# Row terms of the attention scores: GpSimd products and ScalarE sums in place of single-column TensorE products

## The reference, cut to what matters

```
c  = layernorm(x)                                   # 8 batches x 64 tokens x 512 features
cq = einsum('bcd,bqd,d->bcq', c, q, w_cq) + b_cq    # q: 8 x 512 x 512
s  = (c @ w_c + b_c)[:, :, None] + (q @ w_q + b_q)[:, None, :] + cq
a  = softmax(s, axis=2)                             # over q
c2q_att = einsum('bcq,bqd->bcd', a, q)
b_att = softmax(max(s, axis=2), axis=1)             # over the tokens
q2c_att = einsum('bc,bcd->bd', b_att, c)[:, None, :]
z = concat([c, c2q_att, c * c2q_att, c * q2c_att]) @ W_l.T + b_l
```

## Time and profile before

| what | value |
|---|---|
| median of 3 runs | 463.41 us (462.15 to 463.58) |
| the profiled execution's own time | 460.11 us |
| its span, first to last instruction | 458.3 us |
| TensorE busy | 431.9 us, 94% of the span |
| VectorE, ScalarE, GpSimd busy | 277.6, 162.8, 50.9 us |
| mean granted clock of TensorE | 0.985 |

### The profile page before, as it was taken

How to read it: one execution, slowest core, us unless ns; L and a number is a source line. 1 busy time by engine, 2 the same in 40 slices (tenths; PEclk the granted TensorE clock), 3 DMA queues, 4 the chain that set the end, 5 groups by cost and what they waited for, 6 DMA issues and landing times.

```text
span 458.3 us, 8060 instructions
## 1 busy us (share of the span) xinstructions
PE 431.9 (94%) x3103; PEld 310.7 (68%) x3112; DVE 277.6 (61%) x552; ACT 162.8 (36%) x316; POOL 50.9 (11%) x59
## 2 busy tenths in 40 slices
PE   1999999999999999999998999999999999999991
PEld 1666566689898899977467766666666666666660
DVE  5759697673454224488678866654456664446637
ACT  4335234123332114432335432355533355533100
POOL 1300000003221111110203300000000000000064
PEclk9999999999999999997999999999999999999996
DMA  7998795006999766006033769999999999984454
GB/s 266 403 387 327 255 415 201 1 1 250 407 406 405 278 239 246 3 1 245 34 124 154 222 190 375 371 305 338 342 349 361 359 352 327 344 314 146 169 156 137
DMA packets 52382, 116.95 MB, mean 255 GB/s; under 512 B 4834, under 2 KB 4850, under 8 KB 52352
## 3 DMA queue, kind: packets, MB, share of 16 engines
q1 hardware_dynamic: 25984, 67.12, 38.6%
q10 hardware_dynamic: 24800, 44.62, 27.9%
q0 software_dynamic: 1568, 4.79, 3.2%
HBM read 93.98 MB, written 21.50 MB: 252 GB/s over the span
## 4 chain that ended last, share of the span: by engine, by line
PE 88%; DVE 6%; DMA 2%; issue 2%; ACT 1%; POOL 1%; DVEq 0%; ACTq 0%; POOLq 0%
PE banks L1793 19%; PE banks L1559 10%; PE banks L1770 6%; PE banks L1772 6%; PE banks L1771 6%; PE banks L1420 4%; PE banks L1642 3%; PE banks L1422 3%; PE banks L1407 3%; PE banks L1459 3%; PE banks L1421 3%; PE banks L1388 3%; PE banks L1782 2%; PE banks L1592 2%; PE banks L1539 2%; PE banks L1541 2%
## 5 line engine op out<-in xcount | busy, mean ns | idle before, releaser
L1793 PE MATMUL banks<-w,A 128*128 128x512 f32 x208 | 91.6, 592 | 0.0
L674 ACT ACTIVATE A<-banks,b_sb 128x128 f32<-128x128 f32 x112 | 30.5, 384 | 110.7 <-issue 76.7
L1793 PEld LDWEIGHTS banks<-w,A 128*128 128x128 f32 x208 | 38.5, 190 | 43.1 <-issue 43.0
L1292 DVE COPY A<-banks 128x512 f32<-128x512 f32 x28 | 18.0, 686 | 66.9 <-PE banks L1772 66.7
L1220 DVE TENSOR_TENSOR w_lo<-w,w_hi 128x1024 fp32r<-128x1024 f32 x48 | 55.4, 1216 | 0.0
L607 ACT ACTIVATE w_hi<-w 128x1024 fp32r<-128x1024 f32 x48 | 47.3, 1089 | 1.1 <-ACT A L674 0.8
L1559 PE MATMUL banks<-A,w 128*128 128x128 f32 x384 | 46.6, 277 | 0.0
L1559 PEld LDWEIGHTS banks<-A,w 128*128 128x128 f32 x384 | 44.1, 192 | 0.8
L1770 PE MATMUL banks<-w_hi,xr 128*128 128x512 f32 x100 | 40.1, 401 | 0.6 <-DVE xr L1237 0.6
L1771 PE MATMUL banks<-w_lo,xr 128*128 128x512 f32 x104 | 40.5, 389 | 0.0
L1772 PE MATMUL banks<-w_hi,xr 128*128 128x512 f32 x100 | 39.0, 390 | 0.0
(11 more groups left out here) (288 smaller groups left out, 738.2 us busy)
## 6 DMA issues: line engine op xcount, KB each, us to landing
w<-in_w SPq DMA_DIRECT2D x12, 2048.0 KB, 10.1
w<-in_w ACTq DMA_DIRECT2D x12, 2048.0 KB, 10.4
rows_dram<-att ACTq DMA_DIRECT2D x1, 14592.0 KB, 43.0
A<-in_ctxT SPq DMA_DIRECT2D x8, 1024.0 KB, 10.3
A<-in_ctx SPq DMA_DIRECT2D x8, 1024.0 KB, 9.2
w<-in_w SPq DMA_DIRECT2D x6, 1024.0 KB, 5.2
rows_dram<-A ACTq DMA_DIRECT2D x13, 256.0 KB, 3.3
w<-in_wlT SPq DMA_DIRECT2D x3, 1024.0 KB, 14.8
```

Source lines behind the costliest of these rows:

```text
L674: ins = nc.scalar.activation(hT[:, u, f, :], HT[f // 4][:, tile(f % 4)], ACT.Gelu, bias=b1_sb[:, u, f:f + 1])
L1793: ins = mm(YP[:, :], hT[:, u, f, :], w2[:, u, f * D:(f + 1) * D], start=(f == 0), stop=(f == FT - 1))
```

## The change

GpSimd loads `w_c` once as a row on all 128 partitions (256 KB). For each tile it multiplies the normed tile `cn` by it into a scratch that lies in the later `wqkv` buffer. ScalarE sums each scratch tile along its row with an Identity activation in place and its accumulator. VectorE's `token_sums` takes that sum. TensorE's `row_terms` is gone, and with it one 2 KB load on ScalarE's queue. The sum of tile 0 stands between `widen_first` and `copy_cT(0, 1)`; the sums of tiles 1 to 3 stand together between `high_wl(7)` and `exp_scores(1)`. The four products stand on GpSimd ahead of its parameter loads. The `wqkv` load, whose buffer holds the scratch, waits for the four sums too.

```diff
-SCORE_PARAMS = 4
+SCORE_PARAMS = 3
...
+        wc_row, wc_terms = A2[:, 7680:8192], wqkv_flat[:, 3072:5120].rearrange("p (t d) -> p t d", t=NT)
...
             sp.wait_ge(first_psum, NT)
+            sp.wait_ge(rows_summed, NT)
             sp.dma_start(wqkv[:, :, :], ...
...
-            act.dma_start(wc[:, :], t["wcT"]).then_inc(score_params_in, 16)
...
+            def sum_row_terms(n):
+
+                act.wait_ge(terms_ready, n + 1)
+                nc.scalar.activation(wc_terms[:, n, :], wc_terms[:, n, :], ACT.Identity,
+                                     accum_out=row_sum[:, n:n + 1]).then_inc(rows_summed, 1)
...
             widen_first()
+            sum_row_terms(0)
             copy_cT(0, 1)
...
             high_wl(7)
+            for n in range(1, NT):
+                sum_row_terms(n)
             exp_scores(1)
...
+            pool.dma_start(wc_row, t["wc"].to_broadcast([P, D])).then_inc(wc_in, 16)
+            pool.wait_ge(wc_in, 16)
+            for n in range(NT):
+                pool.wait_ge(normed, n + 1)
+                nc.gpsimd.tensor_tensor(wc_terms[:, n, :], cn[:, n, :], wc_row, ALU.mult).then_inc(terms_ready, 1)
+
             pool.wait_ge(s_psum, 1)
...
-                dve.wait_ge(r_psum, n + 1)
+                dve.wait_ge(rows_summed, n + 1)
                 dve.wait_ge(nmax_ready, n + 1)
-                link(nc.vector.scalar_tensor_tensor(msum[:, n:n + 1], nmax[:, n:n + 1], -1.0, MI[:, 0:1],
+                link(nc.vector.scalar_tensor_tensor(msum[:, n:n + 1], nmax[:, n:n + 1], -1.0, row_sum[:, n:n + 1],
...
-            def row_terms(n):
-
-                if n:
-                    pe.wait_ge(q2c_taken, n)
-                else:
-                    pe.wait_ge(score_params_in, 16 * SCORE_PARAMS)
-                for k in range(KT):
-                    ins = mm(MI[:, 0:1], cT[:, k, tile(n)], wc[:, k:k + 1], start=(k == 0), stop=(k == KT - 1))
-                ins.then_inc(r_psum, 1)
...
-            row_terms(0)
...
-            row_terms(1)
...
-                    row_terms(n + 1)
```

More of the change, by code:

```diff
@@ L80, in perceiver_kernel @@
         slot_row = before
-        wcq = sb("wcq", [P, KT]); wq = sb("wq", [P, KT]); wc = sb("wc", [P, KT])
+        wcq = sb("wcq", [P, KT]); wq = sb("wq", [P, KT])
         scal = sb("scal", [P, 3]); bsum = sb("bsum", [P, 1])
@@ L162, in perceiver_kernel @@
         nmax = sb("nmax", [P, NT]); asum = sb("asum", [P, NT]); arec = sb("arec", [P, NT])
-        msum = sb("msum", [P, NT])
+        msum = sb("msum", [P, NT]); row_sum = sb("row_sum", [P, NT])
         mT = sb("mT", [1, 2, S]); mmax = sb("mmax", [1, 2]); msb = sb("msb", [1, 2])
@@ L223, in perceiver_kernel @@
         first_psum = sem("first_psum")
+        wc_in, terms_ready = sem("wc_in"), sem("terms_ready")
         wqkv_in, conv_in, wo_in, params_in = map(sem, ("wqkv_in", "conv_in", "wo_in", "params_in"))
@@ L230, in perceiver_kernel @@
         consts, pool_step = sem("consts"), sem("pool_step")
-        dve_step, act_step = sem("dve_step"), sem("act_step")
+        dve_step = sem("dve_step")
         normed, var_ready, root_ready = sem("normed"), sem("var_ready"), sem("root_ready")
         cT_psum, cT_ready, cw_ready = sem("cT_psum"), sem("cT_ready"), sem("cw_ready")
-        s_psum, nmax_ready, exp_done, r_psum = map(sem, ("s_psum", "nmax_ready", "exp_done", "r_psum"))
+        s_psum, nmax_ready, exp_done, rows_summed = map(sem, ("s_psum", "nmax_ready", "exp_done", "rows_summed"))
         aT_psum, aT_ready, cq_psum, c2q_ready = map(sem, ("aT_psum", "aT_ready", "cq_psum", "c2q_ready"))
@@ L1848, in _ @@
                 ins.then_inc(last_psum, 1)
-_NAMES = ["x", "ctx", "ctxT", "wcqT", "wqT", "wcT", "b_cq", "b_c", "b_q", "wlT", "b_l", "wqkvT", "qkv_bT", "convT",
+_NAMES = ["x", "ctx", "ctxT", "wcqT", "wqT", "wc", "b_cq", "b_c", "b_q", "wlT", "b_l", "wqkvT", "qkv_bT", "convT",
           "conv_bT", "woT", "out_b", "gateT", "w1", "b1T", "w2", "b2"]
@@ L1868 @@
         "ctxT": np.asarray(ctx_1024).transpose(0, 2, 1),
-        "wcqT": by_feature(L0_xattn_w_cq), "wqT": by_feature(L0_xattn_w_q), "wcT": by_feature(L0_xattn_w_c),
+        "wcqT": by_feature(L0_xattn_w_cq), "wqT": by_feature(L0_xattn_w_q), "wc": np.asarray(L0_xattn_w_c).reshape(1, D),
         "b_cq": np.asarray(L0_xattn_b_cq).reshape(1, 1), "b_c": np.asarray(L0_xattn_b_c).reshape(1, 1),
```

## The result

The changed kernel takes 466.00 us (median of 6 runs, 465.35 to 467.17) against 462.96 us (6 runs, 461.87 to 463.58) on the same chip: ratio 1.007, 95% interval 1.0052 to 1.0088, slower by 3.0 us. The forecast was +0.5 us. Its range of 461.8 to 465.8 missed the median by 0.2 us, and 0.63 stood on "within 0.3%". The profiled execution took 466.0 us, its span is 464.2 us.

A forecast was written before the change was run, and what follows sets the result against it. TensorE was 88% of the chain, but a load set `scores(3)`. Delays 0.4 + 0.7 + 0.35 less tile 3's 0.98 gave +0.47 us on 460.11; adding 3.30 for the median gave 463.9 us, range 461.8 to 465.8.

The forecast's parts named there:

- part 6: Loads from `attend(1)` to `scores(3)`: the queue runs at its full rate, so `ctxT(3)` is delayed by as much as `attend(1)`.
- part 1: Products removed from TensorE, 2.94 us at most: tile 1's becomes some 0.4, tile 2's nothing, tile 3's the full 0.98 us.
- Rival D: TensorE idle from 20.1 to 22 us drops its clock to 0.50, costing 3 us more: 466.9; chance 0.05.
- the signs to look for: Expected in the profile after: TensorE idle over 1 us before 22 us and 0.6 before `att` transposes; `scores(3)` waiting over 1.
- Part 4, product 0: GpSimd's first product, 9.2 to 10.4 us, delays `low_part(0, 0)`; it or the row's load makes `scores(0)` late: +0.4 us.
- Part 4, products 1 to 3: GpSimd products from about 17.4 us, 3.45 us together, hold up VectorE's `low_part(0, 1)` and so TensorE: +0.7 us.
- Part 2, the sums: Three ScalarE sums ahead of `exp_scores(1)`, 0.65 us each: tile 1's saving gone and 0.35 us lost.
- parts 3 and 5: ScalarE's sum for tile 0, and the later `wqkv` and GpSimd parameter loads: all free.
- The sum at `attend(1)`: Delays of 0.4, 0.7 and 0.35 us add to +1.45 us at `attend(1)` and at `scores(3)`.
- Rival C: GpSimd-VectorE lock decides everywhere, hold-ups 1.1 + 1.5: +2.6 us, 466.0; each half alone about +1.4; with halves, chance 0.22.
- A: Rival: GpSimd's products do not hold VectorE up; -0.6 to -0.2 us, 463.0; chance 0.24.
- B: Rival: saving counts in full, no hold-up, `ctxT(3)` load moves with TensorE; -1.7 us, 461.7; chance 0.07.

The follow-up runs named there:

- e18: The changed kernel with the 16-byte-a-partition SBUF tile `wc` back in its old place, unused; 463.74 us against 462.74, ratio 1.0024.
- e5: The changed kernel with nine useless 128x512 products on TensorE ahead of its wait for `ctxT(3)`; 464.61 us against 461.56, ratio 1.0073.
- e19: The kernel before with the tile `wc` allocated behind the large tiles instead of ahead of them; 463.49 us, ratio 1.0037.
- e17: The changed kernel with the unused input `wcT` kept in the DRAM input list, no instruction differing; 465.01 us against 461.49, ratio 1.0091.
- e1: The kernel before with only GpSimd's row load and four products added, results unused; 462.87 us against 462.15, ratio 1.0006.
- e2: The kernel before with only ScalarE's four sums added, taken over `cn`, unused; 462.68 us against 462.15, ratio 1.0003.
- e9: The change remade: tile 0's row terms on TensorE, the other tiles' products and sums in idle time, tile `wc` back; 461.80 us against 462.18, ratio 1.0000.
- e12: The kernel before, unchanged, run again for a second profile; 461.79 us against 462.15, ratio 0.9993.
- e13: The kernel before with TensorE's row terms of tiles 1 to 3 left out, nothing in their place; 461.47 us against 461.56, ratio 0.9998.
- e16: e9 with five useless 128x512 products on TensorE ahead of its wait for `ctxT(3)`; 460.53 us against 461.49, ratio 0.9989.
- e3: The changed kernel with GpSimd's products 1 to 3 held back until VectorE's idle time; 464.84 us against 462.15, ratio 1.0046.
- e4: The changed kernel with `low_part(0, 1)` reading its tile from PSUM instead of the SBUF copy; 465.39 us against 461.56, ratio 1.0093.
- e8: The changed kernel with `exp_scores(1)` ahead of ScalarE's three sums; 464.75 us against 461.49, ratio 1.0089.
- e15: The changed kernel, unaltered, run again for a second profile; 464.27 us against 461.49, ratio 1.0071.
- e6: The changed kernel without the loads of `ctxT(3)`, `scores(3)` computing on old data; 463.26 us against 461.56, ratio 1.0028.
- e10: e9 with the load of `wqkv` issued ahead of `ctxT(2)`; 463.16 us against 462.18, ratio 1.0020.
- e11: The kernel before with only the load of `wqkv` moved ahead of `ctxT(2)`; 464.96 us, ratio 1.0069.
- e14: e13 with the load of `wqkv` issued ahead of `ctxT(2)`; 462.69 us, ratio 1.0016.

## Why the prediction was wrong

With the tile back (e18) the changed computation costs +1.0 us by the medians (interval -0.2 to +2.5), which agrees with the forecast's own range of -0.2 to +1.3. Part of that agreement is luck: in the profile e18 is 1.26 us late at first fill, not 0.47. What the stage loses beyond that in the changed kernel's profile stands in two steps. That they are the whole of the +3.0 at the end is not shown, as e5 says.

1. **"What delays `attend(1)` delays `ctxT(3)` by as much" (part 6).** It was delayed by 1.94 at issue and by 3.05 at landing. The 1.1 us between them is a longer flight, 16.3 us against 15.2. The rate of 409 GB/s, which I took over from the earlier trace rows, became 388, and that alone is worth 0.3 us over the 2 MB of `ctxT(3)` (an estimate from the two rates); the other 0.8 was there when `wqkv` landed, 16.8 us after its issue instead of 16.0. The cause is a line of the change that I priced at nothing without saying so: the removed tile `wc`. Put back, it returns 0.9 of the 1.1 us (e18); taken from the kernel before, it costs 0.6 (e19). e17 rules out DRAM. Every profile with the tile in its place had a rate of 406 to 409 GB/s (before, e1, e2, e9, e12, e13, e16, e18), every one without it 386 to 394 (after, e3, e4, e5, e8, e15, e17, e19), on one chip too (e1, e2, e12 and e18 against e3 and e19); in e6, e10, e11 and e14 other loads stand in that stretch.

2. **Tile 2's saving "brings TensorE to `scores(3)` earlier, where it waits for `ctxT(3)`: nothing" (part 1).** The wait was right and "nothing" was wrong. It grew from 0.21 to 2.14 us, and behind it the clock stood at 0.50 while `scores(3)` ran: +1.65 us. Rival D had this mechanism, and put it at 20 to 22 us with a chance of 0.05 (it did happen there in e6 and e15); the signs to look for named a wait "over 1 us" ahead of `scores(3)`, and the two were not brought together. e5 shows in one profile that without the idle time there is no fall. Both steps add up: 0.98 of saving and 1.1 of slower loading, less some 0.1 by which `attend(2)` came later than these, make the 2.14 us out of 0.21.

Step by step, the rest:

- *Part 4, product 0.* The row landed at about 10.4, not 9.2 (6.9 us from issue, not 5.6), and missed `low_part(0, 0)`. It held `low_wl(1)` by 0.88 us instead, a place I had not looked at; through `normed` this moved products 1 to 3 about 1 us later. `scores(0)` came at +0.74 (forecast +0.4) and is in all that follows. It was not the hold-up of `low_part(0, 0)`: e2 has as much without GpSimd. The load's share was right in mechanism: `ctxT(0)` lands 0.79 us later (forecast 0.64), and in e18 and e3 (16.52) `scores(0)` waits for it.
- *Part 4, products 1 to 3.* Right in mechanism. They took 4.13 us, not 3.45 (1.38 each beside VectorE, 1.25 alone in e9; my 1.15 was too low), and the hold-up was 1.03 us, not 0.7. TensorE was idle 2.23 us before the projection, as foretold "over 1 us". Whether it comes hangs on tenths of a microsecond: the same order of instructions gave 0.69 us in e5 and e17.
- *Part 2, the sums.* 0.61 us each (forecast 0.65), costing 0.16 net of tile 1's saving (forecast 0.35), with TensorE idle for 0.25 us ahead of the transposes (foretold 0.6): right in mechanism, a little too high.
- *Part 1, tile 3's 0.98 us, and parts 3 and 5:* right, nothing else is seen at those places.
- *The sum at `attend(1)`:* +1.94 against a forecast of +1.45: a miss of 0.5, small beside the 1.1 and 1.65 behind it.

Rival C gave 466.0, the number measured, by a way that did not happen: `attend(1)` was late by 1.94, not by 3.55. By its own terms each half of C gives +1.2 to +1.3, not +1.4; nothing hangs on it. A and B are refuted in this profile by the 1.72 us row and the 2.14 us wait. Taken at the medians, e18 says that about +1.0 is the change's own work and about +2 the shift with what follows from it (the two were not measured side by side, and their intervals just touch: 0.9995 to 1.0054 and 1.0052 to 1.0088). The shift by itself, in e19, costs 0.4% (0.1 to 0.65).

What stays open. Why nine fillers (e5) bring the stage 2 us and the mean clock back, and the end of the kernel not: at a mean clock of 0.985 e5's median is 464.6, and three runs of e15 at 0.985 lie at 463.7. Why the clock fell behind waits of 1.68 (e3), 2.10 (e15), 2.14, 2.18 (e4) and 3.01 us (e11), and held behind 1.14 (e13), 1.22 (e9), 1.24 (e18), 1.67 (e8), 1.92 (e17), 2.19 (e14) and 2.30 us (e10): the length of the wait alone does not decide. At tile 1's projection it is the same: a fall behind 1.97 (e6) and 2.00 us (e15), none behind 2.02 (e18) and 2.23 us (the changed kernel). And e8, whose profile has no fall behind the wait, is as slow in its median as the changed kernel. The profile is one run: it took 463.87 us at a mean clock of 0.985, while four of the six runs were at 0.981 and took 464.65 to 467.26; so it is for e17 (463.77 at 0.984; three of six at 0.981, 466.24 to 466.76). Whether a fall at this place makes that difference, no trace of those runs says. Which of the shifted tiles slows the loads, and why by such a small shift, was not separated.

## What to carry to other kernels

Where the chain has a wait for a load, time taken off the engine ahead of it only lengthens an idle stretch. Price that stretch by the clock that the next instructions may get. Read a diff for what it does to the allocation too; a tile of 16 bytes a partition, removed or moved, changed the load rate in one stretch of this kernel by 5%, and a spare tile in its place is the cheapest experiment there is. Ahead of moving work to GpSimd, list every two-input VectorE operation from the earliest to the latest moment at which the work can start, not the one that the estimate hits.

## What the runs showed of the hardware

- With a tile of 16 bytes a partition removed from ahead of the large SBUF tiles, two 1 MB loads in a row ran at 386 to 394 GB/s instead of 406 to 409, at a DMA share of 1.03 to 1.05 either way (both ways round in e18 and e19).
- A GpSimd product of 128x512 takes 1.25 to 1.28 us alone. A VectorE subtraction with two SBUF inputs that starts while it runs is held (0.69 becomes 1.35 to 1.72; 1.23 becomes 1.96 to 2.26), one with a PSUM input is not (0.69). Where VectorE starts first, even by 0.09 us, it keeps its 0.69 us and the product waits (1.95 us in e1).
- Sixteen products of `scores` take 3.65 us at a granted clock of 1.00 and 5.30 to 5.35 where it falls to 0.50 behind a wait of 1.68 to 3.01 us, in the unchanged computation as well (e11).
